# Edge pass of a graph network: four places for the row picked from the table on the chip, and the sums of group s-2 issued after the second layer of group s-1

## The reference

```python
msg = concatenate([x[dst], x[src] - x[dst]], axis=-1)   # 64 wide, per edge
h = relu(msg @ W1 + b1)                                 # 64
h = relu(h @ W2 + b2)                                   # 128
h = relu(h @ W3 + b3)                                   # 64
m = h @ W4 + b4
x = layernorm(x + segment_sum(m, dst) / maximum(count, 1))
```

## Time and profile before

| | |
|---|---|
| median of three runs | 6016.44 us |
| span of the profiled execution | 6035.8 us (the page gives no time of its own around it) |
| edge pass, first `rows_in` to last | 99.6 to 1196.8 us: 103 steps between 104 groups |
| busy over the whole span | PE 85%, DVE 61%, ACT 29%, POOL 64% |

### The profile page before, as it was taken

The page is one execution under the profiler, slowest core; times in us unless marked ns, Lnnn a source line. Parts: engine busy times, 40 slices in busy tenths (PEclk is TensorE's granted clock), DMA queues, the critical chain, the costliest instruction groups (busy, mean ns, idle before and its releaser), DMA issues.

```text
span 6035.8 us, 146385 instructions
## 1 busy us (share of the span) xinstructions
PE 5102.4 (85%) x51654; PEld 3499.3 (58%) x51654; DVE 3709.3 (61%) x7059; ACT 1751.6 (29%) x3755; POOL 3865.9 (64%) x4026
## 2 busy tenths in 40 slices
PE   4888888868886888769999995899999859999996
PEld 3666666668886888725555554455555535555554
DVE  6444444478788888746566556556566655656666
ACT  3222222245553000023333331333333223333331
POOL 3666666557774777567777761777777347777770
PEclk8888788879898999979999997899999979999998
DMA  4555455423332333234554442445444324444441
GB/s 103 138 137 137 132 147 138 131 73 88 86 87 69 95 93 97 67 89 123 125 128 123 123 115 57 104 125 125 125 123 125 95 59 124 124 122 124 123 125 56
DMA packets 689583, 661.13 MB, mean 110 GB/s; under 512 B 398676, under 2 KB 481051, under 8 KB 688859
## 3 DMA queue, kind: packets, MB, share of 16 engines
q1 hardware_dynamic: 555562, 484.42, 27.2%
q0 software_dynamic: 128960, 166.69, 15.1%
q10 hardware_dynamic: 4336, 0.67, 0.1%
HBM read 562.12 MB, written 89.17 MB: 108 GB/s over the span
## 4 chain that ended last, share of the span: by engine, by line
PE 63%; issue 16%; DVE 12%; POOL 5%; DVEq 3%; ACT 1%; ACTq 1%; DMA 1%; POOLq 0%
PE ps L1027 17%; PE ps L871 12%; PE ps L966 8%; POOL rows L372 5%; PE ps L987 4%; PE ps L835 4%; PE ps L818 3%; PE ps L1001 3%; PE ps L946 2%; PE ps L977 2%; PE ps L886 2%; PE ps L803 2%; PE ps L826 1%; DVE acc L1465 1%; DVE region L1452 1%
## 5 line engine op out<-in xcount | busy, mean ns | idle before, releaser
L372 POOL DMA_INDIRECT rows<-table,idx x2340 | 2247.6, 960 | 1120.4 <-issue 713.1
L1027 PE MATMUL ps<-region,hot 128*128 128x272 f32 x4992 | 1324.2, 409 | 190.1 <-DVE region L1702 84.7
L1027 PEld LDWEIGHTS ps<-region,hot 128*128 128x128 f32 x4992 | 916.4, 194 | 494.0 <-issue 293.1
L636 ACT ACTIVATE region<-ps 128x512 f32<-128x512 f32 x1248 | 677.3, 595 | 1680.9 <-PE ps L966 1680.9
L1734 DVE TENSOR_TENSOR acc<-acc,ps 128x272 f32 x1248 | 545.4, 437 | 891.4 <-PE ps L1027 775.4
L359 POOL DMA_INDIRECT rows<-table,idx x728 | 706.9, 971 | 432.8 <-PE ps L807 220.4
L871 PE MATMUL ps<-hot,region 128*128 128x192 bf16 (+1 forms) x8640 | 859.9, 260 | 63.9 <-DVE region L1568 56.7
L871 PEld LDWEIGHTS ps<-hot,region 128*128 128x128 bf16 x8640 | 785.1, 103 | 79.0 <-DVE region L1568 61.7
L1724 DVE TENSOR_TENSOR region<-ps,region 128x1056 f32<-128x1056 f32 x624 | 777.5, 1252 | 49.0 <-issue 44.8
L966 PE MATMUL ps<-xT,wcat 64*128 64x512 f32 x2496 | 714.6, 649 | 9.3 <-ACT region L636 9.3
L384 POOL DMA_INDIRECT rows<-table,idx x480 | 460.4, 959 | 242.4 <-issue 143.5
(11 more groups left out here) (302 smaller groups left out, 6765.3 us busy)
## 6 DMA issues: line engine op xcount, KB each, us to landing
hot<-hot_dram SPq DMA_DIRECT2D x624, 256.0 KB
turned<-turned_dram SPq DMA_DIRECT2D x624, 128.0 KB
rows<-table,idx POOLq DMA_INDIRECT x3548
hot_dram<-hot SPq DMA_DIRECT2D x104, 512.0 KB
region<-hot_dram SPq DMA_DIRECT2D x90, 512.0 KB
xwin<-table SPq DMA_DIRECT2D x1664, 24.0 KB
region<-d_dram SPq DMA_DIRECT2D x104, 256.0 KB
turned_dram<-turned SPq DMA_DIRECT2D x104, 256.0 KB
```

What stands on the lines that cost most here:

```text
L372: pool.indirect_dma_start(rows[:, n % 2, j, :], None, table, bass.IndirectOffsetOnAxis(ap=idx[:, s:s + 1], axis=0)).then_inc(rows_in3[n % ...
L636: act.activation(rz[g % 2][:, 2 * t + side, :], ps[:, Z + side, :], ACT.Relu).then_inc(rz_made, 1)
L1027: mm = pe.matmul(ps[:, AG + i, 0:PC + H], hot[:, b, 4 * side + 2 * i + j, :], px[b][:, 4 * side + 2 * i + j, :], start=(j == 0), stop=(j = ...
```

## The change

`one0` moves to a free stretch of another buffer (columns 2064 to 2191 of `region1`) and gets four places; `pick0(g)` then waits for `x0_made` of g-3, the end of `rows_in(g-4)`. On PE `second_layer(s-1)` is issued before `sums(s-2)` and no longer after it. Nothing is computed in another way, and the counts of instructions stay as they are.

```diff
-        one0 = o0[:, 6544:6544 + 2 * C].rearrange("p (b c) -> p b c", b=2)
+        one0 = o1[:, 2064:2064 + 4 * C].rearrange("p (b c) -> p b c", b=4)
@@ rows_in
-                                pe.matmul(ps[q:q + C, 0, at], one0[:, b, :], ident[:, :], start=True, stop=True)
+                                pe.matmul(ps[q:q + C, 0, at], one0[:, g % 4, :], ident[:, :], start=True, stop=True)
@@ pe_pass0
                 if s + 2 < G:
                     read_one(s + 2)
+                if 0 <= s - 1 < G:
+                    second_layer(s - 1)
                 if s >= 2:
                     sums(s - 2)
-                if 0 <= s - 1 < G:
-                    second_layer(s - 1)
                 if s < G:
                     rows_in(s)
@@ pick0
-                if g >= 2:
-                    v.wait_ge(x0_made, g - 1)
-                v.tensor_reduce(one0[:, g % 2, :], cand0.rearrange("p g c -> p c g"), AX.X, ALU.add).then_inc(one0_kept, 1)
+                if g >= 4:
+                    v.wait_ge(x0_made, g - 3)
+                v.tensor_reduce(one0[:, g % 4, :], cand0.rearrange("p g c -> p c g"), AX.X, ALU.add).then_inc(one0_kept, 1)
```

## The result

The changed kernel takes 5827.05 us, the median of four runs (5813.10 to 5835.78), against 6014.88 us of the kernel before beside it. The ratio is 0.9693, with a 95% interval of 0.9672 to 0.9714: 188 us faster and 5827 us, where 165 us and 5851 us were forecast.

The account below looks back on a forecast made before the run. A ring of waits through PE and DVE was taken to bound the edge pass at 10.65 us a step. With POOL's 8.94 plus 0.1, taken as 9.05, (10.65 - 9.05) x 103 = 165 us: 6016.4 to 5851 us, range 5815 to 5928.

Parts of the forecast that it names:

- the ring over the place: Edge pass, PE and DVE: `rows_in`, reduction, additions, relu, `sums`, `second_layer`, `rows_in` again; left at 6.3 to 7.6 us.
- DVE's wait at line 1446: DVE's reduction waits for `rows_in` to free its place: 414.1 us, 4.27 us a time; expected to go.
- PE's at line 835: PE's wait before `sums` for DVE's relu: 98.9 us in total, expected under 20 us.
- POOL sets the pace: Edge pass: seven gathers and gaps on POOL take 8.94 us a step and become the bound; chance 0.58.
- The 0.1 for stretches in which PE falls behind by more than the buffers hold: Edge pass: 0.1 us a step added to POOL's 8.94, for PE lagging beyond POOL's three buffers.
- h: Share of edge-pass time PE spends at half clock: 0.30 before, expected 0.2 to 0.3 after.
- The new wait I named: PE before `rows_in`, for POOL's gathered rows: about 0.9 us, only in steps at full clock.
- The clock rival: PE's wait before `rows_in` brings more clock falls: 11.2 us a step, 53 us lost, 6070 us; chance 0.04.
- the 9.21 of the prediction: Edge pass: length in us of the PE and DVE ring in one step with everything at its fast duration.
- the wait before line 826: PE's wait for ACT's relu of the second layer: 18.8 us, 0.19 a step, ended by the swap.
- late transfers: SP's stores land late and delay DVE's `turned0`: 9.7 us a step, 98 us gained, 5918 us; chance 0.09.
- DVE shutting POOL out for whole instructions: `turned0` and `stationary0` on DVE cost POOL their full length: 9.41 us a step, 5889 us; chance 0.06.

Follow-up runs that it names:

- six gathers: One of seven gathers left out per group: kernel before 6000.94 us (0.9984), changed kernel 5726.12 us (0.9516), places alone 5760.64 us (0.9601), swap alone 5797.36 us (0.9667).

## Why the prediction was right, point by point

The mechanism was right: the ring over the place opens, DVE's wait at line 1446 and PE's at line 835 vanish, and POOL sets the pace. The run on the kernel before with six gathers (no change) and the one on the kernel after (about 100 us) show the change of the bound from both sides. A step was put at 9.05 and is 8.73. The 0.32 us are three terms, all in the same direction:

- POOL's pace. I took 8.94, seven times what a gather and its gap took before. It is 8.86, since a gather takes 0.961 us and not 0.970: fewer of them are made long by line 1417 or 1434 (46 of 633 against 90 of 673).
- The lead. I multiplied by 103 steps, but POOL starts the pass three groups ahead and issues only 101 in it: 895 us instead of 913 at the same pace. That is the 0.13 between 8.86 and 8.73. (The trace of either kernel has 21 gathers, three groups, ahead of the first `rows_in`.) This was in the code (three buffers) and I missed it.
- The 0.1 for stretches in which PE falls behind by more than the buffers hold. They do not occur: POOL does not wait for PE from 150 us to the end of the pass. I had h between 0.2 and 0.3, and it is 2 x (1 - 0.93) = 0.14.

The new wait I named is there, but not in most steps: 45.2 us in 29 waits over 800 us, 0.5 us a step. PE alone at full clock does a step in 7.69 us, so it uses up POOL's lead within some steps, then waits, then has a step at a lower clock, in which POOL gets its lead back. From 575.9 us on the steps take 7.69, 7.96, 8.43, 10.54 and 12.30 us, the last with a mean clock of 0.60, and then 7.69 again. The clock rival's mechanism can be seen at close range. PE in the changed kernel waits 1.96 us for gathered rows behind `sums`, and the third and first layer after it run at 1.2 GHz (granted clock 0.50 from 522.5 to 528.1):

```profile
517.22 2.00 PE L835 MATMUL ps<-region,hot 128*128 128x65 f32 x16
521.18 0.22 PE L803 MATMUL ps<-identb,rows 128*32 128x128 bf16 x1 [1.96 <-DMA rows<-table,idx]
...
522.58 3.68 PE L826 MATMUL ps<-w,region 128*128 128x64 f32 x16
526.05 2.02 PE L813 MATMUL ps<-xT,w 128*128 128x512 f32 x2
```

As argued, such a fall costs POOL's pace nothing: POOL has no wait for PE there. One price in that rival was off: 11.2 us a step would lose 57 us and not 53. The wait was also not always shorter than the 1.15 of before, as I had argued against that rival; the longest is 5.2 us.

Where the gain came from is the point I had not laid out; in the prediction the clock was only a condition. Filling the wait took a step from 10.65 to 9.70 without opening the ring, and paid for its twelve matmuls out of that, so the clock is worth at least 0.95 of the 1.92 us. The trace of before gives another figure: 26 of its 103 steps ran wholly at a granted clock of 1.00, with the ring closed, and they took 9.41 us in the mean (the 9.21 of the prediction is one step without `stationary0`). By this the clock is 10.65 - 9.41 = 1.24 us and the ring, down to where POOL takes over, 0.68. That is an estimate, since those 26 need not be like the others in all else. So half to two thirds of the gain is the clock coming back, and the opened ring is what brought it.

The swap I held to be worth 0.19 us a step, the wait before line 826. That was wrong for the swap by itself: it also takes 1.06 us out of the ring, which alone is enough. In the forecast it did no harm, since POOL caps both. That the total came out near is therefore no support for my reading that the places bring the gain and the swap next to nothing.

Of the rivals, late transfers showed a little (line 1417 waits 14 times and 22.8 us in 800 us, against 7 times and 11.2 in 1040) without reaching the end. DVE shutting POOL out for whole instructions didn't appear, and a second such operation in each step didn't bring it; what there is costs 0.2 us, and mainly where the operation starts 0.1 to 0.2 us ahead of the gather.

## What to carry to other kernels

When one engine waits for a buffer place and another then waits for it, write the ring out with its durations and compare it with what each engine needs by itself: every edit that takes the ring below the next bound is worth the same, and the second one nothing, until that bound is moved too: with six gathers both parts are clearly better than either. To price a loader that runs ahead, count the groups it still has to issue, not the steps. And before a wait on TensorE is valued at its own length, look at the granted clock behind it.

## What the runs showed of the hardware

Adding 12 matmuls a step to TensorE, in a wait of about 1 us, made the kernel 85 us faster: the granted clock of the stretch rose from 0.85 to 1.00. The busy share of a stretch does not give its clock: TensorE was busy for 94% with a clock of 0.93 in the changed kernel (753.17 of 800 us), and for 92% with a clock of 1.00 in the filled one (828.75 of 900). Busy time is longer at the lower clock, and the changed kernel has single waits of up to 5.2 us.

An indirect gather issued by GpSimd took 0.94 us with neither line 1417 nor line 1434 of VectorE beside it. It took 1.14 to 1.15 us in the mean where one of these, about 0.5 us long, had started 0.1 to 0.2 us before it, and over 1.05 us each time (109 of 109 gathers in the traces of before and after).
